# Attention masks moved off the matrix engine: eight extra contraction rows for the far keys, products on the exponentials for the near ones

## The reference

```python
xn = layernorm(x)
q, k, v = xn @ Wq, xn @ Wk, xn @ Wv          # 16 heads of 16; 8 key and value heads, each for 2 heads
mask = causal & (i - j < 128 | lm[j])        # lm: landmark tokens, see below
p = softmax(q k^T / 4 + where(mask, 0, -10000))
s = (p v) @ Wo
h = gelu(xn @ ternary(w1)^T + b1)            # 1024 wide
g = silu(h @ ternary(w2)^T + b2)
out = x + s * g
```

## Time and profile before

| | |
|---|---|
| median of three launches | 735.6 us (735.58 to 736.71) |
| profiled execution, its own time | 737.96 us |
| its span | 736.3 us |
| PE busy, instructions | 628.7 us (85%), 4336 |
| ACT busy | 475.7 us (65%), 723 |
| DVE busy | 375.4 us (51%), 1002 |
| POOL busy | 74.7 us (10%), 92 |
| mean granted clock of PE | 0.935 of full speed |

### The profile page before, as it was taken

One profiled execution on the slowest core, in us unless ns is written; L12 is line 12 of the kernel. 1 busy time (PEld: TensorE's weight loads), 2 busy tenths in 40 slices (PEclk: granted clock), 3 DMA queues, 4 the chain that ended last, 5 costly groups with the idle time before them and its releaser, 6 DMA issues. The chain is left out here.

```text
span 736.3 us, 11753 instructions
## 1 busy us (share of the span) xinstructions
PE 628.7 (85%) x4336; PEld 351.7 (48%) x4336; DVE 375.4 (51%) x1002; ACT 475.7 (65%) x723; POOL 74.7 (10%) x92
## 2 busy tenths in 40 slices
PE   0537809999999989999999679999999899799982
PEld 0524604664455546654554536654554556334532
DVE  7968961665827434767454615648364521410101
ACT  1112417677877766697768556697768666888680
POOL 4000020020010201020100301110100210201001
PEclk9968957999999979999999869999999899899997
DMA  7000699000145659001190756001082691030101
GB/s 214 0 0 1 83 89 153 9 8 20 47 62 77 73 116 144 16 8 31 35 124 21 83 143 102 11 8 58 16 115 37 80 137 42 7 90 8 52 10 49
DMA packets 46833, 43.84 MB, mean 60 GB/s; under 512 B 6065, under 2 KB 41394, under 8 KB 46770
## 3 DMA queue, kind: packets, MB, share of 16 engines
q1 hardware_dynamic: 44642, 41.18, 33.6%
q10 hardware_dynamic: 2128, 1.84, 0.8%
HBM read 11.28 MB, written 4.19 MB: 21 GB/s over the span
## 5 line engine op out<-in xcount | busy, mean ns | idle before, releaser
L812 ACT ACTIVATE probs<-sc_ps,shift 128x512 f32<-128x512 f32 (+1 forms) x288 | 175.8, 617 | 102.0 <-PE sc_ps L725 101.3
L718 PE MATMUL sc_ps<-q_stack,k_stack 99*128 99x512 bf16 (+3 forms) x768 | 198.5, 344 | 33.3 <-PEq L189 14.7
L815 ACT ACTIVATE probs<-sc_ps,key_bias 128x1024 f32<-128x1024 f32 (+3 forms) x256 | 204.9, 818 | 16.5 <-PE sc_ps L718 15.8
L738 PE MATMUL att_ps<-probs,v_sb 128*32 128x512 f32 (+3 forms) x1536 | 167.4, 508 | 0.0
L718 PEld LDWEIGHTS sc_ps<-q_stack,k_stack 99*128 99x128 bf16 x768 | 50.2, 99 | 182.9 <-issue 70.8
L725 PE MATMUL sc_ps<-near_mask,mask_ident 128*128 128x256 bf16 (+1 forms) x576 | 105.1, 266 | 0.0
L850 POOL TENSOR_TENSOR h_lo<-hid,h_hi 128x512 fp32r<-128x512 f32 x32 | 43.2, 1350 | 342.3 <-DVE h_hi L882 342.3
L725 PEld LDWEIGHTS sc_ps<-near_mask,mask_ident 128*128 128x128 bf16 x576 | 56.4, 103 | 37.5 <-issue 7.1
L665 PE MATMUL aux_ps<-w2T,h_hi 128*128 128x256 f32 x256 | 70.1, 307 | 0.0
L665 PE MATMUL aux_ps<-w2T,h_lo 128*128 128x256 f32 x256 | 63.2, 279 | 0.0
L773 ACT ACTIVATE hid<-aux_ps,b_sb 128x512 f32<-128x512 f32 x64 | 42.9, 687 | 22.8 <-PE aux_ps L655 13.8
(11 more groups left out here) (152 smaller groups left out, 748.9 us busy)
## 6 DMA issues: line engine op xcount, KB each, us to landing
q_stack<-q_parts SPq DMA_DIRECT2D x96, 128.0 KB, 8.1
k_stack<-k_parts SPq DMA_DIRECT2D x24, 256.0 KB, 8.8
xn<-in_L_attn_hidden_states SPq DMA_DIRECT2D x4, 1024.0 KB, 8.2
attT<-att_raw SPq DMA_DIRECT2D x128, 32.0 KB
rden_bc<-den SPq DMA_DIRECT2D x64, 64.0 KB
probs<-in_L_ffn_w SPq DMA_DIRECT2D x2, 1024.0 KB, 7.8
out_y<-xn SPq DMA_DIRECT2D x4, 512.0 KB, 6.1
xn<-in_L_attn_hidden_states SPq DMA_DIRECT2D x3, 512.0 KB, 4.0
```

The costliest lines, as they stand in the source:

```text
L718: last = pe.matmul(sc_ps[:, 2 * u + hh, lo:CH], k_stack[0:KROWS + SHIFT_ROWS, h // REP, kb * P:(kb + 1) * P], q_stack[0:KROWS + SHIFT_ROWS ...
L738: last = pe.matmul(att_ps[32 * q:32 * q + 32, n % 2, lo:CH], v_sb[:, kb, j * VW:j * VW + 32], probs[:, i % 3, q, lo:CH], start=(kb == 0), ...
L812: last = act.activation(probs[:, i % 3, us, lo:near], sc_ps[:, us, lo:near], ACT.Exp, bias=shift[:, 0:1], scale=HD ** -0.5)
L815: last = act.activation(probs[:, i % 3, us, near:CH], sc_ps[:, us, near:CH], ACT.Exp, bias=key_bias[:, kb:kb + 1], scale=HD ** -0.5)
```

## The change

The old code is kept as `general_path` for inputs that need exact maxima, with its own buffers. The flag is read once, after `set_up`, and all turns of the usual case are in `fast_path`. There:

1. The eight rows 96 to 103 of the contraction hold the far mask: in `q_stack` row r is 32768 for the query blocks at least 2 after block r, else 0 (`later_tile`); in `k_stack` row r is 0 for landmark keys of block r, else -1 at that block's keys (`far`). The three rows of shift and `key_bias` are gone, and so is the matmul of `mask_ident`.
2. `exps(i)` is one instruction for a pair, over all columns from `lo`, with the bias `shift`.
3. The near masks act on `probs` after the exp: POOL's `causal(i)` (affine_select on the diagonal block of four heads) in the 32 steps that have one; `local(i)`, a product with `near`, in the steps that have the block behind it: 12 on DVE in the first half, 16 on POOL in the second.
4. `values(i)` runs three steps behind (`BEHIND` = 3) with four buffers of `probs`.
5. `q_stack` holds three groups of four heads instead of all of q. It is refilled group by group by SP (`fill_q`: 7 transfers, once the scores of the group that used the slot are done), and `k_stack` two key heads at a time (`fill_k`: 6 transfers, four times a turn), with `fill_far` at the end.
6. A small block before the first turn fills the constant tiles, which were filled in the set-up. Reciprocal roots on DVE are cut into pieces that are spread over several steps, and the layer norm begins two steps earlier.

```diff
-                            if near > lo:
-
-                                first = 0 if has_tri(i) else kb + 1
-                                end = kb + 2 if has_local(i) else 1
-                                for hh in range(2):
-                                    last = pe.matmul(sc_ps[:, 2 * u + hh, lo:near], mask_ident[:, :], near_mask[:, first:end:kb + 1, :],
-                                                     start=False, stop=True)
+                                    last = pe.matmul(sc_ps[:, 2 * u + hh, lo:CH], k_stack[0:KROWS + T, h // REP, kb * P:(kb + 1) * P],
+                                                     q_stack[0:KROWS + T, SLOT[n], 2 * u + hh, lo:CH], start=True, stop=True)
@@ values(i) on PE @@
                                 pe.wait_ge(exp_done, 2 * (i + 1))
+                                if has_tri(i):
+                                    pe.wait_ge(tri_done, TRIS[i])
+                                if has_local(i):
+                                    pe.wait_ge(local_done, LOCALS[i])
@@ exps(i) on ACT @@
-                            if near > lo:
-                                last = act.activation(probs[:, i % 3, us, lo:near], sc_ps[:, us, lo:near], ACT.Exp,
-                                                      bias=shift[:, 0:1], scale=HD ** -0.5)
-                            if near < CH:
-                                last = act.activation(probs[:, i % 3, us, near:CH], sc_ps[:, us, near:CH], ACT.Exp,
-                                                      bias=key_bias[:, kb:kb + 1], scale=HD ** -0.5)
-                            last.then_inc(exp_done, 1)
+                                    act.activation(probs[:, i % NPROB, us, lo:CH], sc_ps[:, us, lo:CH], ACT.Exp,
+                                                   bias=shift[:, 0:1], scale=HD ** -0.5).then_inc(exp_done, 1)
@@ causal and local on POOL; local on DVE is the same @@
+                            def causal(i):
+                                c, _, kb = STEPS[i]
+                                block_probs = probs[:, i % NPROB, :, (kb - TC * c) * P:(kb - TC * c + 1) * P]
+                                pool.wait_ge(exp_done, 2 * (i + 1))
+                                pool.affine_select(out=block_probs, in_=block_probs, compare_op=ALU.is_ge, fill=0.0, base=0,
+                                                   pattern=[[0, NQ], [1, P]], channel_multiplier=-1).then_inc(tri_done, 1)
+
+                            def local(i):
+                                c, _, kb = STEPS[i]
+                                block_probs = probs[:, i % NPROB, :, (kb + 1 - TC * c) * P:(kb + 2 - TC * c) * P]
+                                pool.wait_ge(exp_done, 2 * (i + 1))
+                                pool.tensor_tensor(block_probs, block_probs, near[:, kb, :].unsqueeze(1).to_broadcast([P, NQ, P]),
+                                                   ALU.mult).then_inc(local_done, 1)
@@ fill_q on SP @@
+                            def fill_q(n):
+                                c, g = n % NG // GROUPS, n % GROUPS
+                                if main:
+                                    sp.wait_ge(sc_done, 2 * (GROUP_END[FREED_BY[n]] + 1))
+                                if n >= NG or not main:
+                                    sp.wait_ge(q_split, QT * c + g // QT + 1)
+                                cs = slice(c * CH, (c + 1) * CH)
+                                for i in range(NPART):
+                                    sp.dma_start(q_stack[i * HD:(i + 1) * HD, SLOT[n % NG], :, :],
+                                                 q_parts[half_rows(g), g // QT, QPART[i], cs]).then_inc(q_in[SLOT[n % NG]], 16)
+                                sp.dma_start(q_stack[KROWS:KROWS + T, SLOT[n % NG], :, :],
+                                             later_tile[:, cs].unsqueeze(1).to_broadcast([T, NQ, CH])).then_inc(q_in[SLOT[n % NG]], 16)
@@ copy of a q projection on ACT @@
-                            if main and kind == "q_proj":
-                                act.wait_ge(stack_in[1], 16 * NPART * QT)
+                                    if main and kind == "q_proj":
+                                        for slot in range(3):
+                                            act.wait_ge(q_in[slot], 16 * (NPART + 1) * SLOT[3:GROUPS * (a[1] + 1)].count(slot))
```

2273 lines of the change are left out of this document (1481 added, 792 removed).

## The result

The changed kernel takes **703.15 us** in the median of four launches (702.14 to 703.92), the one before 735.59 (735.49 to 736.71). The ratio is 0.9555, 95% interval 0.9538 to 0.9572: 32.7 us less. 701 had been forecast, by a sum of 34.4.

The account below looks back on a forecast made before the run. PE was taken as the bound, ACT close behind. Three turns with preparation at 9.0 us and the last at 7.4 gave 34.4 off 737.96; with the launches' median 2.4 lower, 701 us, 8 in 10 between 682 and 724.

Parts of the forecast that it names:

- Mask matmuls: Mask matmul pairs gone from PE's score steps: 14.3 us a turn at most, less 1.0 for ACT's pace.
- seven of the eight halves: Halves of the main turns where what PE issues inside a step was said to be worth nearly its own length.
- Near masks: Charges for POOL's waits, DVE beside POOL and the turns' ends, near masks acting after the exp: 17.3 us.
- POOL's burst in the last turn: Last turn's second half: PE's values wait for POOL's selects and products in three groups with few jobs, 3.9 us.
- DVE beside POOL: Second halves: the engines hinder each other and PE waits for DVE in the projections, 1.5 us a turn with preparation.
- POOL's residual needs that x, and values(27) come three steps later, which covers it.: Step 27: x, reloaded behind the k refill, was to reach POOL's residual in time, at no charge.
- Refills: Step 26: ACT's copy of the third q projection waits for the last group's refill, 0.5 us a turn with preparation.
- Set-up: Set-up and first turn: earlier thresholds (8.4 us) against jump and constant fills (10) and other terms; taken as 0.
- Three steps behind: Values a step later with four buffers: said to move nothing within a half.
- POOL sets the pace: Rival: the select costs 1.35 us, so waits for POOL grow in 16 groups; 24 us less gain, 725; chance 0.12.
- Clock: Rival: waits for POOL bring PE's lower clock back inside the second halves; 12 us, 713; chance 0.06.
- rival in series: Second halves: DVE and POOL wait for each other on every instruction; 738; chance 0.06, with other stalls of like size.

Follow-up runs that it names:

- b1: The changed kernel without any near mask: no selects or products on POOL and DVE and no waits for them; 688.4 us.
- d1: The changed kernel with only x for the residuals issued ahead of the k refill on SP, POOL's order kept; 712.2 us.
- a3: The changed kernel with x for the residuals issued ahead of the k refill and POOL's residuals behind the near masks of their step; 697.9 us.
- b3: The kernel before without the mask matmuls and with each exp in one piece, near and far masks not applied; 692.1 us.
- a2: The changed kernel with ACT's copy of a q projection waiting only for the refills that read that part of q_parts; 699.3 us.
- a1: The changed kernel with the layer norm of the next image's x at steps 5, 9 and 12 in place of 3, 7 and 10; 708.1 us.
- c1: The changed kernel with the edits of a2 and a3, and the next image's x as the first transfer of a turn; 692.2 us.
- c2: The changed kernel with the values two steps behind the scores in place of three, four buffers kept; 729.9 us.

## Why the prediction was right, step by step

The forecast was met in the total. Term by term:

- **Mask matmuls, 14.3 a turn less 1.0 for ACT's pace.** Too large. 57.2 - 4 = 53 was charged, 41.9 measured, 44.9 with the merged exps. The pair's length by PE's starts and its worth in the half with preparation were read rightly (6.1 of 7.0). The step that failed is to carry that to "seven of the eight halves": the first halves gave 21.0 of 29.2, the last turn's first only 3.9 of 7.3, where PE came to wait for exps and the clock was lower.
- **Near masks, 17.3 in all.** Measured 15.3, so right as a sum and wrong in its parts. POOL's burst in the last turn: 3.9 charged, 72.2 - 70.9 = 1.3 measured, of which 0.2 is a wait for POOL and 1.1 PE's busy time, at a granted clock of 0.95 for 0.98. The last select on the path at the end: 23.2 us against 22.4 in b1, 0.8 where 2.0 was charged. DVE beside POOL: 1.5 a turn charged, nothing by itself. In place of them stands the circle of residual, product and near mask, 3.8 us a half with the lower clock that it brought in turn 2, which I had not seen: I counted what is queued behind PE's wait, and not what is queued behind POOL's.
- **"POOL's residual needs that x, and values(27) come three steps later, which covers it."** In after they didn't cover it (2.12 us at 191.55). But with the x in time (d1) the kernel was slower: what holds PE is the order of POOL's queue (a3 against d1).
- **Durations.** The select: 0.75 taken, 0.64 typical, 0.73 in the mean, as the estimate from the earlier trace rows had it at its lower end. The product: 1.35 taken, 1.16 typical, 1.18 in the mean.
- **Refills.** 0.5 a turn charged. The halves of b1 are 1.9 us longer than those of b3, and ACT's wait for the DMA is enough for it (6.9 us in the three turns of b1, 5.3 in after). 1.7 a half came back in a2, part of it clock.
- **Layer norm two steps earlier.** Not priced at all, though the diff shows it. DVE's wait for the x had to be asked for, with what is queued behind it. Without it turns 1 and 2 were 2.9 and 2.1 us shorter in a1, 2.3 and 1.3 in c1.
- **Set-up.** 0 taken, 4.0 gained. The threshold came at 16.94 for about 17, 8.3 us earlier. The jump and the block that fills constants had been put at 10; the first `ffn_up` block begins 3.5 us earlier than before, so they and all else of that stretch cost 4.8. The low end of the bound (4) was nearer.
- **Three steps behind.** 0 taken; without it 27 us are gone (c2). The rivals had "POOL sets the pace" at 725: that is about where the kernel with the values two steps behind came out (729.9), though there the first halves lose as much.
- **Stage times.** First halves "near 34": 34.5 in turn 0, 36.8 to 41.9 in the others. These were longer in the kernel before, too (41.9 to 49.5 for 40.6). For the half with preparation I wrote 79.5; my own charges (7.0 - 1.0 - 1.3 - 1.5 - 0.5) give 82.2, so that figure wasn't what the sum rests on. Measured 83.8 in the mean.
- **Clock.** The rival had the lower level back inside the second halves, behind waits for POOL, for 12 us. It came, but small: once, in turn 2 (0.98 for 1.00 before), 1.5 to 1.7 us of PE's busy time. The last turn's second half has 0.95 for 0.96. In d1 the lower level came back in all three halves, which is 4.0 of its 9 us.

So the total was met within 2 us by errors of both signs, which is in part luck. Forecast: 53.2 for matmuls and exps, less 1.5 for refills, 0 for set-up and all else, less 17.3 for the near masks, is 34.4. Measured by the ladder b3, b1, after: 44.9, plus 3.1 for set-up, refills and all else of the frame, less 15.3, is 32.7. In the 3.1 is a gain that the prediction left out: the stretches between main turns are 1.0 to 1.2 us shorter each in b1 than in b3. The `If` that stood there is gone; it was counted for turn 0 alone, and no run shows it apart.

## What to carry over

When work moves to an engine with room, its busy share says little; look at what stands in that engine's queue between the producer and the new instruction, and at whom that waits for. The thing that the critical engine needs goes first in the queue. And a wait of 15 us for a transfer in front of a late instruction is not yet its cause: with the transfer early, the next wait in the circle took its place, and the clock fell behind it. So when a stage gets longer, compare the critical engine's busy time and its granted clock as well as its waits.

Before a step is moved earlier, ask when its input lands; before it is moved later, ask what it runs into.

## What the runs showed of the hardware

- Some instructions of DVE and POOL shut each other out, up to the length of a whole instruction. DVE instructions on 9 columns took up to 1.11 us beside POOL's select and product, 0.17 alone, and one on 2 columns took 6.30 beside a fill. It goes the other way too: a select of 0.64 us took 1.15 when DVE's product had begun 0.05 us before it (after, turn 1):

```profile
254.91 0.69 DVE L1632 TENSOR_TENSOR f_probs<-f_probs,f_near 128x512 f32<-128x512 f32 x1 [2.44 <-ACT f_probs L1551]
```
```profile
254.96 1.15 POOL L1592 TENSOR_SCALAR_AFFINE_SELECT f_probs<-f_probs 128x512 f32<-128x512 f32 x1 [7.02 <-ACT f_probs L1551]
```

- The Trainium skill ("SBUF — State Buffer", section "Who interferes with whom") has both kinds: a DVE instruction with two SBUF inputs against a GpSimd instruction that reads SBUF, and DVE's two-port modes against any. By that rule, the traces agree: the roots' steps with two inputs were held by select and product, and the one-input instruction on `thr` (6.30 us) by a fill that reads nothing, while its neighbour out of PSUM took 0.16 us at 17.00, inside the fill that began at 16.54. So "the instructions with one SBUF input go through", as the prediction's rival in series has it, is too wide: `thr` has one and was held. Whether it ran in a two-port mode, no row shows. The price for the kernel is in the runs: 4.1 us of DVE's time a half and none of the kernel's, until a queue's order brought it onto the path.
- PE's clock fell to its lower level inside second halves at the end of single waits, or just behind them: 2.74 us (after, turn 2), 2.89 (c2, turn 0) and 3.70 (d1, all three), each time with half-speed matmuls behind it. Not every such wait did it: c2's of 2.90 and 2.94 us in turns 1 and 2 left those halves at 1.00.
- A select of 128x512 in float32 costs POOL 0.64 us, and a product of that size 1.16.
